# Row maxima moved by GpSimd instead of by transfers, and relative rows two tiles earlier, in a two-layer transformer kernel

## The reference

```python
def _L1_attn_ref(x, Wq, Wk, Wv, Wo, E):      # H = 16 heads of 8, G = 4 key groups
    q = (x @ Wq.T).reshape(B, T, H, hd).transpose(0, 2, 1, 3)
    k = jnp.repeat((x @ Wk.T).reshape(B, T, G, hd), r, axis=2).transpose(0, 2, 1, 3)
    v = ...
    q = q * (1.0 / hd) ** 0.5
    scores = jnp.einsum('bhqd,bhkd->bhqk', q, k)
    dist = jnp.clip(pos[None, :] - pos[:, None], -127, 127) + 127
    bias = jnp.einsum('bhqd,kqd->bhqk', q, E[dist])
    attn = jax.nn.softmax(scores + bias, axis=-1)
    out = jnp.einsum('bhqk,bhkd->bhqd', attn, v)
    return out.transpose(0, 2, 1, 3).reshape(B, T, D) @ Wo.T
```

## Time and profile before

| | |
|---|---|
| median of 3 runs | 1604.02 us (1601.19 to 1611.08) |
| the profiled execution | 1608.73 us, of it the span 1607.0 us |
| busy in the span | PE 84%, DVE 56%, ACT 50%, POOL 41% |
| second attention, about 959 to 1538 us | 512 ScalarE exponentials of 596 ns (L862), 256 VectorE tiles (L764 855 ns, L765 513 ns), 256 shifts on GpSimd (L842 563 ns) |
| turn of the maxima, L713, 128 rows and 128 columns | 64 x 223 ns |
| off-band matmul, L690, 75 rows and 512 columns | 336 x 397 ns |

### The profile page before, as it was taken

How to read it: one execution, slowest core, us unless ns; L and a number is a source line. 1 busy time by engine, 2 the same in 40 slices (tenths; PEclk the granted TensorE clock), 3 DMA queues, 4 the chain that set the end, 5 groups by cost and what they waited for, 6 DMA issues and landing times. The chain is left out here.

```text
span 1607.0 us, 37860 instructions
## 1 busy us (share of the span) xinstructions
PE 1354.1 (84%) x14415; PEld 900.8 (56%) x14415; DVE 892.9 (56%) x2426; ACT 809.7 (50%) x1571; POOL 664.3 (41%) x1281
## 2 busy tenths in 40 slices
PE   3999999989999996226999158999989999999957
PEld 1567777747777776214767124555545555555545
DVE  4556666446666665670233255566666776666652
ACT  2455555545555553100232254676666777767643
POOL 1456666516666661026154413333333444333300
PEclk9999999989999997557999666999898999999978
DMA  5610000053000000712154336666666666665500
GB/s 182 96 22 2 3 2 2 2 108 51 2 2 2 2 2 1 260 53 72 29 107 77 60 100 190 188 204 197 185 174 184 197 186 181 177 170 174 162 2 27
DMA packets 112816, 154.21 MB, mean 96 GB/s; under 512 B 15011, under 2 KB 98339, under 8 KB 111339
## 3 DMA queue, kind: packets, MB, share of 16 engines
q1 hardware_dynamic: 105851, 146.91, 32.8%
q0 software_dynamic: 6784, 4.87, 2.2%
HBM read 84.98 MB, written 66.46 MB: 94 GB/s over the span
## 5 line engine op out<-in xcount | busy, mean ns | idle before, releaser
L435 ACT ACTIVATE t_Pt<-t_psT 128x512 f32<-128x512 f32 x512 | 278.9, 595 | 233.8 <-PE t_psT L329 233.8
L377 DVE CUSTOM_DVE_ANT_0 t_Z<-t_psS,a0b_L 128x1024 f32<-128x1024 f32 x256 | 310.2, 1220 | 149.7 <-issue 146.7
L862 ACT ACTIVATE t_Pt<-t_psT 128x512 f32<-128x512 f32 x512 | 288.0, 596 | 176.5 <-PE t_psT L677 100.1
L764 DVE TENSOR_REDUCE t_mm<-t_psS 128x1 f32<-128x640 f32 (+1 forms) x256 | 218.9, 855 | 129.2 <-DMA t_A<-relative_rows 97.7
L400 POOL TENSOR_SCALAR t_Z<-t_Z,t_m 128x1024 f32<-128x1024 f32 x256 | 287.6, 1123 | 0.0
L329 PE MATMUL t_psT<-idf,t_Z 128*128 128x128 f32 x2048 | 278.4, 280 | 10.8 <-POOL t_Z L400 7.3
L329 PEld LDWEIGHTS t_psT<-idf,t_Z 128*128 128x128 f32 x2048 | 223.0, 143 | 101.3 <-issue 55.2
L663 PE MATMUL t_psS<-a1b_KT,a1b_QT 72*128 72x512 bf16 (+3 forms) x672 | 214.4, 348 | 14.6 <-DVE t_mm L765 14.1
L706 PE MATMUL t_psO<-t_Pt,t_Vh 128*32 128x128 f32 x4096 | 171.0, 286 | 4.3 <-DVE t_Os L788 3.9
L288 PE MATMUL t_psS<-a0b_KT,a0b_QT 72*128 72x512 bf16 x512 | 155.1, 385 | 5.1 <-PEq L76 3.3
L833 POOL TENSOR_SCALAR t_neg<-t_m 128x4 f32<-128x4 f32 x64 | 14.2, 223 | 320.8 <-DVE t_m L774 320.8
(11 more groups left out here) (329 smaller groups left out, 1477.3 us busy)
## 6 DMA issues: line engine op xcount, KB each, us to landing
relative_rows<-t_rows SPq DMA_DIRECT2D x256, 192.0 KB, 2.7
t_A<-relative_rows SPq DMA_DIRECT2D x192, 192.0 KB, 3.0
t_A<-relative_rows SPq DMA_DIRECT2D x64, 128.0 KB, 2.6
a1b_QT<-query_parts SPq DMA_DIRECT2D x24, 192.0 KB
x_B<-in_b SPq DMA_DIRECT2D x1, 4096.0 KB, 18.8
x_A<-in_a SPq DMA_DIRECT2D x1, 4096.0 KB
a0b_QT<-query_parts SPq DMA_DIRECT2D x6, 576.0 KB
a0b_KT<-key_parts SPq DMA_DIRECT2D x18, 192.0 KB
```

The lines of the kernel that those rows point to most:

```text
L377: nc.vector.tensor_tensor_reduce(out=Z[:, j, :], in0=psS[:, j % 2, :], in1=L[:, qt, :], scale=1.0, scalar=3e38, op0=ALU.add, op1=ALU.min, ...
L435: nc.scalar.activation(Pt[:, qt % 2, j, half * (N // 2):(half + 1) * (N // 2)], psT[:, half, :], ACT.Exp).then_inc(s_exp, 1)
L764: v.reduce_max(mm[:, u % AR, 1:2], psS[:, u % 2, width:N], AX)
L862: nc.scalar.activation(Pt[:, q % PR, :], psT[:, unit_item(G, i) % RR, :], ACT.Exp).then_inc(s_exp, 1)
```

## The change

Each of the 12 turned rows of maxima now gets a contraction row of its own, 96 to 107, so that nothing has to move across partitions. `turn_max` turns a t_mp of 27 x 4 columns, of which the first 96 are zero, so that the maxima come out on partitions 96 to 107; VectorE copies them there; GpSimd writes them into QT for four heads at once, multiplied by t_own_col, which is one for the row's own head and zero for the others. The three transfers per group and their semaphores are gone. L690 contracts 108 rows. The rows 72 to 95 of QT are zero and the rows 72 to 107 of KT are one; both are filled once by four transfers in `between`, from two DRAM tensors that the first phase writes. The relative rows of a tile are made, stored and fetched two tiles earlier: `AHEAD` is 14, where it was 12. The stores of the second batch's query and key parts move from the end of `project_pair` into the first three groups of the attention, and the loads of later heads stand one group earlier.

```diff
+MR = 3 * P // 4
+KM = MR + 4 * SPLIT
 ...
-                store(1, s_parts, s_parts)
 ...
+    AHEAD = 3 * J + 2
+    rel_at = lambda u: rel_item((u - AHEAD) // J, (u - AHEAD) % J)
 ...
-        mp = ph.sb("mp", [P, ZR, SPLIT, J], BF16)
+        mp = ph.sb("mp", [P, ZR, MR // J + SPLIT, J], BF16)
+        own_col = ph.sb("own_col", [P, J], BF16)
 ...
                     if kt == off(qt)[0]:
-                        pe.wait_ge(s_md[G % 2], 48 * (G // 2 + 1))
+                        pe.wait_ge(s_mq, G + 1)
 ...
-                for G in range(-3, GROUPS):
+                for G in range(-4, GROUPS):
 ...
-                        if i % 2 and G + 3 < GROUPS:
-                            relative(G + 3, i // 2)
+                        if i % 2 and 0 <= G * J + i // 2 + AHEAD < TILES:
+                            relative(G * J + i // 2 + AHEAD)
 ...
-                    v.tensor_copy(mr[0:SPLIT * J, G % 2, :], psT[0:SPLIT * J, extra_item(G - 1) % RR, 0:P // 2].bitcast(BF16)).then_inc(s_me, 1)
+                    v.tensor_copy(mr[MR:KM, G % 2, :], psT[MR:KM, extra_item(G - 1) % RR, 0:P // 2].bitcast(BF16)).then_inc(s_me, 1)
 ...
                         g.tensor_scalar(zb, zb, 1.0, neg[:, z, j:j + 1], ALU.mult, ALU.add).then_inc(s_sub, 1)
 
+                    pool.wait_ge(s_sub, (G + 1) * J)
+                    pool.wait_ge(s_me, G + 1)
+                    g.tensor_tensor(QT[MR:KM, b, hq * J:(hq + 1) * J, qt * P:(qt + 1) * P], spread(mr[MR:KM, G % 2, :].unsqueeze(1), [KM - MR, J, P]),
+                                    spread(own_col[MR:KM, :].unsqueeze(2), [KM - MR, J, P]), ALU.mult).then_inc(s_mq, 1)
+                    pool.wait_ge(s_mq, G + 1)
 ...
-                def max_rows(G):
-                    b, hq, qt = G // PB, G % PB // QT_N, G % QT_N
-
-                    sp.wait_ge(s_me, G + 1)
-                    for s in range(SPLIT):
-                        sp.dma_start(QT[KR + s:KR + s + 1, b, hq * J:(hq + 1) * J, qt * P:(qt + 1) * P], mr[s * J:(s + 1) * J, G % 2, :]).then_inc(s_md[G % 2], 16)
+                def part(n):
+                    i, kr = n // 2, 2 * GKV * DH
+                    if n % 2 == 0:
+                        sp.dma_start(qd[1][i].rearrange("(d h) n -> h d n", d=DH), parts[0][:, i, :]).then_inc(s_parts, 16)
+                    else:
+                        sp.dma_start(kd[1][i, 0:kr, :].rearrange("(d v) n -> v d n", d=DH), parts[1][0:kr, i, :]).then_inc(s_parts, 16)
 ...
-                        u = (G + 3) * J + j
-                        if j == 2 and 0 <= G + 1 < GROUPS:
-                            max_rows(G + 1)
+                        u = G * J + j + AHEAD
+                        if j % 2 == 0 and 0 <= G < 3:
+                            part(2 * G + j // 2)
 ...
+                sp.wait_ge(s_fill, 32)
+                for b in range(B):
+                    sp.dma_start(KT[KR:KM, b].rearrange("p a n -> p (a n)"), fill_k).then_inc(s_one, 16)
+                    sp.dma_start(QT[KR:MR, b].rearrange("p h n -> p (h n)").bitcast(F32), fill_q).then_inc(s_one, 16)
```

More of the change, by code:

```diff
@@ L440, in _, with project_pair @@
                 copy_out(QUADS - 1, 1)
-def project_pair(nc, tag, xn, wq, wk, wv, QT, KT, V, idf, qd, kd, parts, ones, s_one, s_near, s_parts, scale, far):
+def project_pair(nc, tag, xn, wq, wk, wv, QT, KT, V, idf, qd, kd, parts, s_near, scale, far):
     nv = wk.shape[1] // DH
@@ L550, in _ @@
             def _(sp):
[L551 to L560, removed]
+                for i, (s_qp, s_kp) in enumerate(((s_qhi, s_khi), (s_qmid, s_kmid), (s_qlo, s_klo))):
+                    sp.wait_ge(s_qp, 2)
+                    sp.dma_start(qd[0][i].rearrange("(d h) n -> h d n", d=DH), qp[0][:, i, :]).then_inc(s_qd, 16)
+                    sp.wait_ge(s_kp, 2)
+                    sp.dma_start(kd[0][i, 0:kr, :].rearrange("(d v) n -> v d n", d=DH), kp[0][0:kr, i, :]).then_inc(s_kd, 16)
                 sp.wait_ge(s_qd, 16 * SPLIT)
@@ L618, in attend_direct @@
         s_bias = [ph.sem(f"bias{i}") for i in range(AR)]
-        s_md = [ph.sem("md0"), ph.sem("md1")]
+        s_mq = ph.sem("mq")
         s_load = ph.sem("load")
@@ L851, in gather @@
                         act.wait_ge(s_wr[u % 4], 16 * (u // 4))
-                    nc.scalar.activation(rows[:, u % 4, :], psT[:, rel_item(G - 3, j) % RR, 0:REL], ACT.Copy).then_inc(s_rows, 1)
-                for G in range(-3, GROUPS):
+                    nc.scalar.activation(rows[:, u % 4, :], psT[:, rel_at(u) % RR, 0:REL], ACT.Copy).then_inc(s_rows, 1)
+                for G in range(-4, GROUPS):
                     for i in range(QT_N):
@@ L921, in _ @@
                     sp.wait_ge(s_bias[i], 16 * (TILES // AR))
-                for i in range(2):
-                    sp.wait_ge(s_md[i], 48 * (GROUPS // 2))
 def sparse_experts(nc, tag, logits, xr, y, con, wp, wg, wo, W1, W2, primitives, logit_rows, logit_all, xin, ydr, s_init, s_y):
@@ L1716, in _, with between @@
                 sp.wait_ge(s_out, 16 * NCH)
-def between(nc, tag, y, X, xn, ydr, s_y, w, wo, wk2, kb, EBT, wqkv1, wo1, far, band, scratch, zp, idb):
+def between(nc, tag, y, X, xn, ydr, s_y, w, wo, wk2, kb, EBT, wqkv1, wo1, far, band, scratch, zp, idb, QT, KT, fill_q, fill_k, s_fill, s_one):
     BT = BAND // P
     with phase(nc, tag) as ph:
-        ph.sems += s_y
+        ph.sems += s_y + [s_fill]
         stats, agg = ph.sb("stats", [P, 2, NCH, TC, 6]), ph.sb("agg", [P, 2, NCH, TC, 2])
@@ L1945, in sandwich @@
         EBT = ph.sb("EBT", [P, BAND], BF16)
-        between(nc, "m1", y, X, xn, ydr, s_y, w, wo, wk2, kb, EBT, wqkv1, wo1, far, band, scratch, zp, idb)
         with phase(nc, "a1b") as pb_:
```

73 lines of the change are left out of this document (41 added, 32 removed).

## The result

The changed kernel takes 1601.25 us (median of 20 runs, 1594.68 to 1607.62). The kernel before, run beside it, took 1610.26 (20 runs, 1598.68 to 1625.5). The ratio is 0.9951 [0.9933, 0.997]: faster by 0.5%, where 1560 us and 3% had been forecast. The profiled span is 1598.5 us against 1607.0.

A forecast was written before the change was run, and what follows sets the result against it. SyncE's queue was taken as the pace of the second attention, unsteady clock as second loss. Periods 44.0 us shorter, with +2.0 - 1.4 - 0.5, gave 44.1 less: 1564.6 from the profiled 1608.7, so 1560 us by median; range 1545 to 1588.

The forecast's parts named there:

- 63 periods: Second attention, first to last negation of maxima: 554.5 us before, forecast 510.5, as 30.5 for three and 480.0 for 60.
- fills at the start: First phase: two more stores, issued at about 13 us, fit a hole in DMA work or stick out; 0.5 us lost.
- phase boundary: End of the projection: stores of the second half's parts leave it, so the attention begins sooner; 2.0 us gained.
- start: Start of the second attention: two more relative matmuls stand ahead of the first scores; 1.4 us lost.
- That is under 8.0: it stops being the pace.: SyncE's queue in the second attention: without L890 it needs 6.1 us a group, perhaps 6.8, plus loads, under TensorE's 8.0.
- No effect: Rival: SyncE's queue stretches from 6.1 to 8.8 us a group if landings take over 4 us; 1604 us, chance 0.05.
- eight groups at 7.98: Second attention, 1255.51 to 1319.32 us: eight periods of 7.98 us each, cited as evidence against rivals.
- two tiles ahead: SyncE's fetches of t_A: five steps of lead instead of three, about ten us, remove VectorE's 83.5 us of waits nearly whole.
- 8.0 us a group: Second attention: what TensorE needs per group when it is fed, against 8.80 us on average before.
- the multiply becomes the pace: Rival: GpSimd's multiply takes 5.9 us, a period becomes 10.0 us; 76 us more, 1680 us, chance 0.05.
- The turn: TensorE's turn of the maxima, now 108 columns: longer weight load hidden by its waits for ScalarE; nothing added.
- a clock that stays unsteady: Rival on the clock: it stays unsteady after the change; chance 0.06, its size left out of the text given.

The follow-up runs named there:

- e5: Changed kernel with the second batch's query and key rows never stored as parts or loaded during the attention, first batch's rows read instead: 1583.66 us, ratio 0.9835.
- e4: Changed kernel with each step of SyncE's queue fetching tile u-2 instead of u-1: 1568.85 us, ratio 0.9775.
- e8: Kernel before, its three transfers of maxima kept and no fills, with a lead of 14 tiles and tile u-2 fetched instead of u-1: 1561.27 us, ratio 0.9694.
- e1: Changed kernel with the two fills' stores issued in the first batch's first attention instead of the first phase: 1588.85 us, ratio 0.9889.
- e10: e7 with GpSimd's multiply done twice per group: 1549.88 us, ratio 0.9642.
- e11: e7 with GpSimd's multiply done four times per group: 1577.61 us, ratio 0.9808.
- e7: e6 with the maxima turned as 128x12 straight to partitions 96 to 107, instead of 128x108 with zero columns: 1553.56 us, ratio 0.9654.
- e6: Changed kernel with the fills' stores issued at the first attention and tile u-2 fetched instead of u-1: 1558.44 us, ratio 0.9669.

## Why the prediction was wrong

Forecast against the profiled execution: 44.1 us less. Measured: 8.5 less in the span. The 35.6 us between them, by the prediction's own terms:

| term | forecast | measured | difference |
|---|---|---|---|
| 63 periods | 510.5 | 540.4 | +29.9 |
| fills at the start | +0.5 | +12.2 | +11.7 |
| kernel before: its experts' stretch | 0 | -5.5 | -5.5 |
| phase boundary | -2.0 | -2.8 | -0.8 |
| start | +1.4 | +2.2 | +0.8 |
| behind the last group | 0 | -0.5 | -0.5 |

**The step that failed: "That is under 8.0: it stops being the pace."** The queue's need, 6.1 us, was one measured stretch less its L890, with landings of 2.7 us at the median and loads at their issue of 0.3 to 0.6. But 2.7 us is a mixture, and L890 was part of it. SyncE's timeline in the kernel before, right behind the L890 and the store of 1352.77 in the earlier trace rows:

```profile
1354.70 0.32 SPq L883 DMA_DIRECT2D t_A<-relative_rows  x1
1355.11 0.41 SPq L873 DMA_DIRECT2D relative_rows<-t_rows  x1
...
1358.43 0.32 SPq L883 DMA_DIRECT2D t_A<-relative_rows  x1
```

The store behind L890 is fetched after 1.93 us, the one of 1355.11, behind a fetch, after 3.32. Over the whole attention before, the 62 stores right behind L890 land in 1.9 us at the median and the 119 right behind a fetch (those whose landing the trace has) in 3.2. With L890 gone, the store that it had kept apart from the fetch ahead stands behind that fetch like the others: 3.6 us, 5.1 behind the loads of the slow stretch. At 2.7 us a group would need 2 x (0.41 + 2.7) = 6.2; at 3.57 it needs 7.96. So taking L890's 1.8 to 2.4 us out of the queue gave back most of it as longer landings that the next fetch waits for. The prediction had this case among its rivals ("No effect": landings of over 4 us, chance 0.05) and dismissed it by eight groups at 7.98. Those groups had no load in the queue, so they said nothing on those that had. e5 shows the loads' share (seven tenths of the early excess), e4 the whole: with the fetch one tile later both halves run at 8.1. What the prediction gave as the cause of the loss, a late queue, was right; that removing L890 frees it was not.

Two smaller readings belong to it. The prediction took the wait for t_A as the cost and the 141.3 us of SyncE's waits for landings as a sign of a full queue. It was the reverse: a queue that waits 141.3 us is not full, it is blocked, and e8, 3.1% faster with all of L890 in it, shows that unblocking it makes L890 harmless without removing it. And the work done "two tiles ahead" has only four rows buffers behind it: rows can't be made earlier than their buffer's store lands, so the lateness went to ScalarE (42.6 us in the attention, 0 before), then to TensorE through t_psT.

**Fills: 0.5 us.** The DMA engines' empty stretch from 26 us on was the wrong cover: the transfers are issued at 13 us, when these engines are full in the kernel before (DMA share 0.88 and 1.00, next to last number):

```profile
12.00:18.00 6.00, 0.00 (x0) 0.00 (x0) 3.63 (x21) 1.28 (x1) 0.00 (x0) 1.00 0.88 318
18.00:24.00 6.00, 0.00 (x0) 0.00 (x0) 5.50 (x32) 0.21 (x1) 0.00 (x0) 1.00 1.00 330
```

What held up the program is SyncE's issue time, 10.24 and 3.88 us, ahead of a barrier: VectorE's first norm starts right behind it, at 28.43 us, and the first matmul is 13.9 us late. e1 takes 12.4 us back.

**The profiled execution of the kernel before.** From its first indirect transfer at 712.67 us to the start of the projection at 936.32 it took 223.65 us; the changed kernel and e8 took 218.11 and 217.68 for the same code. So 5.5 us of its 1607.0 were that execution's own, and the spans hide by it half of the fills' cost.

**What held.** 8.0 us a group where TensorE is fed: 8.07 in the late half, and 8.09 over 60 periods in e4. That e4's 63 periods come to 509.0 us, so near the 510.5 of the sum, is in part luck: its first three take 23.4 us where 30.5 had been left. The multiply: 1.04 us for 1.17 forecast, off the path (e10), and the onset of the rival "the multiply becomes the pace" where it was put, since a group of GpSimd that passes TensorE's pays the difference (e11: 1577.61 for 1578 expected). The 33 more contraction rows cost nothing: 392 ns at 108, 397 at 75. TensorE's waits for L890 gone. The turn was called hidden; it costs 0.11 us a group in the profiles, some 7 us, which e7 takes back (4.9 us by the medians).

**The clock.** In the changed kernel it hardly moves: 0.51 from 962 to 996 us as before, and 0.98 instead of 0.97 from 996 to 1538. The kernel before has four low stretches there, each shortly behind an idle gap of TensorE: the clock is 0.50 from 1026.5 to 1032.5, 1129 to 1136, 1204 to 1213 and 1409 to 1415 us, and the gaps, of 1.63, 2.02, 1.30 and 1.62 us, end at 1024.01, 1127.83, 1202.09 and 1406.94. Not every gap has one behind it: that of 1.55 us ending at 1507.71 has none. The changed kernel has one low stretch, 0.50 from 1205 to 1217 us, behind a gap of 1.67 us. In e4 no gap of over 1 us and no low stretch lies between 996 and 1500 us, near the attention's end: the clock is 1.00 from 986 to 1500 us (0.99 from 996 to 1515), and 0.64 instead of 0.51 from 962 to 996. The forecast's sum has no term for the clock, and a clock that stays unsteady had a chance of 0.06; no run changes the clock alone, so what it costs by itself is not shown.

**Left open.** Why a load of 24 rows delays the store behind it by more than a fetch does in SyncE's groups 6 to 26 (5.14 us against 3.50) and not in 3 to 5 (3.47): no run changed the load's form or place. Why the first three periods differ so much between the runs (22 to 34 us). More rows buffers, perhaps another cure, were not tried.

## What to carry to other kernels

A queue that waits for its own transfers' landing, as this one did for 141.3 us, is blocked, not full: before taking work out of it, put the dependent transfer one item later and give its consumer the lead for it; here those two edits were worth 3.1%, neither much alone, and the work taken out nothing in the steady groups and some 0.5% in all, not all of it by that work. A median landing can be a mixture (2.7 us here, of 1.9 behind the small transfers and 3.2 behind a fetch): price it for each neighbour ahead in the queue (small transfer, fetch, load) and for each stretch of the program apart, and ask which neighbour the change takes away. A transfer ahead of a barrier can cost its issue time (10.24 and 3.88 us here): price it where it is issued, not where there is room.

## What the runs showed of the hardware

- Landing of a 192 KB store, medians: 1.9 us with over 1 us of free queue ahead of it (e4, 141 stores) and right behind the small transfers of L890 (kernel before, 62), 3.2 to 3.6 right behind a fetch of the same size (kernel before and changed), 5.1 behind a load in the slow stretch (changed kernel, 21). The shortest landing of any of them is 1.8 us (kernel before).
- Issuing can hold the issuing engine for long: 10.24 and 3.88 us for the two fills at 13 us, 0.92 and 38.44 us for the same two at 54 us. Issues of 192 KB stores and fetches mostly take 0.32 to 0.45 us. So the price is not the instruction's alone; it changes with its place in the program. What sets it is not shown: the DMA share was 0.86 from 12 to 18 us in the changed kernel, and 0.54 in e1 during the issue of 38.44 us.
- GpSimd, bf16 multiply of 12 rows by 512 with both inputs repeated by their access pattern: 1.04 us (changed kernel, L849), against 1.17 for f32 128 by 512 without repetition (kernel before, L1815).
- TensorE writes a 12-row result to partitions 96 to 107 directly (e7), in 222 ns and a weight load of 83, against 259 and 127 with 96 columns of zeros ahead (e6).
